# Four graph layers on one core: folding a weight product in the first layer and moving its softmax beside the aggregation

## Chip, cores and metric

One core of one Trainium2 chip runs the whole program. The metric is the time of one execution on the device in microseconds (us).

## What is computed

Four graph layers over N = 1536 nodes of 512 features, each followed by a residual sum and a layer norm. The change is in the first. With A the adjacency counts (24,576 edges and a loop at each node), it is:

```python
node_proj = h @ Wf + bf                       # 1536 x 256
img_proj = img_feats @ Wi + bi                # 36 x 256
logits = tanh(node_proj[:, None] + img_proj) @ Wa + ba
att = softmax(logits, axis=1)                 # 1536 x 36
img = att @ img_feats                         # 1536 x 1024
h1 = h @ Wn + bn
msg = A @ h1 + img @ Wim + bim
out = relu(concatenate([msg, h1]) @ Wap + bap)
x = layernorm(x + out)
```

Then come a relational layer of two steps, five GIN steps and a weighted aggregation, which the change leaves alone.

## The kernel before

Nodes stand in 12 tiles of 128 (`NT`), features in 4 blocks of 128. The program is written by hand, one instruction stream per engine: `block.sync` (SP) issues nearly all DMAs, `block.gpsimd` makes constants, `block.vector` (DVE), `block.scalar` (ACT) and `block.tensor` (PE) compute. Each stream runs in the order of its text and waits on semaphores (`wait_ge`); nothing else sets the order.

First come the edges: 96 windows of 16 nodes, in which one-hot matrices on DVE and products on PE make the adjacency matrices. Beside them the bases of the relational layer come in 64 chunks through four buffers (SP line 317) and are mixed on PE (L1205). The change touches the SP stream's last chunks.

The first layer follows, in four stretches:

1. `x_turned`: x is loaded three tiles at a time, transposed on PE (L1251) and copied to `xt` (L644). `projected` makes node_proj transposed (L1266), DVE copies it to `proj` (L661). ACT squares the rows of x for a bound (L1018). `pbias` holds the image's projection plus the biases.
2. PE makes G = img_feats Wim (L1387), then, per tile, h1 = x Wn (`rows`, L1295). DVE adds bn (L750), and splits h1 into two fp16 halves with a common scale (L752, L754). PE transposes h1 back (L1402), DVE copies it over `xt` (L757), since the output needs h1 as the stationary operand.
3. `aggregate` (L1309): per tile 24 fp16 products sum A h1. DVE scales it and adds bim (L771); PE transposes that message (L1434), DVE copies it (L776), and PE makes the output as own part (L1295) plus message part (L1441) in one bank; DVE adds bap into `xt` (L783).
4. When all lots (below) are summed, softmax for all 1536 nodes: `logit_t` (L787), transposes (L1447), max, exp, sum, transposes back (L1452). Then per tile the attended image, att times (G Wap's upper half), is made in its own bank (L1459), added (L810), relu and residual (L813), statistics (L814, L815), norm (L1064), transposed (L1473), copied (L1069).

The logits are made in 27 lots (`LOTS`): three groups of 512 nodes times nine sets of four image regions. ACT takes tanh of the upper 128 of the 256 features for the four regions (L1049), then of the lower (L1054). DVE's `halves` scales the upper (L733) and adds the lower with its weight (L739). PE's `dots` sums over the partitions (L1377), four products into four strips of 32 rows. `upper` is one buffer, `lower` two. DVE makes one lot per two tiles in stretch 2 and two per tile in stretch 3; PE does the same a tile or more later:

```python
# TensorE, stretch 2, after rows() of tile i and before the transposes of tile i - 1
if i >= 4 and i % 2 == 0:
    dots()
# VectorE, stretch 2, after shift and split of tile i and the copy of tile i - 1
if i >= 2 and i % 2 == 0:
    halves(1)
```

After stretch 4 the relational layer begins with its gates (L1334).

Of the kernel before, what the change touches and what calls it, by code (L numbers as in the profile page):

```python
# [8 lines left out]
P = 128  # L9
N, D = 1536, 512  # L10
NT = N // P
# [19 lines left out]
BB_COUNT = {3: 3, 4: 4, 5: 4, 6: 5, 7: 5, 8: 6}  # L31
MEASURED = (0, 2, 4, 5, 6, 7)
N_SMALL = 5 + 4
# [10 lines left out]
def program(nc, ins, out):  # L44
    with ExitStack() as ctx:
# [20 lines left out]
        wa = sb("wa", [P, 2], F32)  # L66
        pbias = sb("pbias", [P, 2, RG], F32)
# [28 lines left out]
        wim = part(hflat, 0, [8, D])  # L96
        wi = part(hflat, 16384, [8, PJ])
        proj = part(hflat, H1, [2, N])
        x_first = part(hflat, H1, [9, D])
        att_t = part(hflat, H1 + 12288, [N])  # L100
        img = part(hflat, H1 + 18432, [1024])
        g2 = part(hflat, H1 + 18432, [D])
        g_t = part(hflat, H1 + 20480, [4, RG])
        att = part(hflat, H1 + 22528, [NT, RG])
        wf = wb[:, 0, :, 0:PJ]

        adj_flat = [adj[:, m, :, :].rearrange("p j n -> p (j n)") for m in range(3)]
        logit_t = part(adj_flat[2], 0, [N])
        LOGIT = (2, 3, 7)
        LOTS = 3 * 9  # L110
        upper = part(adj_flat[2], 0, [4, 512])
        lower = [[part(adj_flat[2], 8192, [4, 512])], [part(hflat, H1 + 12288, [3, 512]), part(adj_flat[2], 16384, [1, 512])]]

        def lower_of(n, g):

            return lower[n % 2][0][:, g, :] if n % 2 == 0 or g < 3 else lower[1][1][:, 0, :]
# [78 lines left out]
        def static_slots(w):  # L195
# [6 lines left out]
        assert at <= 2 * 2 * NT * D  # L202
# [20 lines left out]
        weights = {k: sem("in_" + k) for k in ("wf", "wi", "img", "wim", "small", "wn", "wt", "wbm", "ts_out", "ts_in", "root", "l1a", "l1b", "aw", "att", "as_out", "as_in")}  # L223
# [9 lines left out]
        upper_ready, lower_ready, upper_scaled, halves_ready, halves_used = [sem(x) for x in (  # L233
            "upper_ready", "lower_ready", "upper_scaled", "halves_ready", "halves_used")]
# [3 lines left out]
        seen_ps, seen_read = sem("attended_ps"), sem("attended_read")  # L238
# [3 lines left out]
        h1_ready, h1t_ps, h1t_cp = sem("h1_ready"), sem("h1t_ps"), sem("h1t_cp")  # L242
        acc_ps, acc_read = sem("acc_ps"), sem("acc_read")
        m_ps, m_cp = sem("m_ps"), sem("m_cp")
# [16 lines left out]
        fin = sem("fin")  # L261

# [48 lines left out]
        def _(sp):  # L311
# [8 lines left out]
            for n in range(3):  # L320
# [9 lines left out]
                (epsc[:, 0:5], ins["L2_gnn_eps"].unsqueeze(0).broadcast_to([P, 5])),  # L330
            ]
# [4 lines left out]
            FIRST_SMALL = 8  # L336
            for n in range(CH):
# [70 lines left out]
            def first_of_l1():  # L408

                for k in range(4):  # L410
                    sp.wait_ge(comb_out[k], 64 * 17)
# [1148 lines left out]
```

## Time and profile before

| | before |
|---|---|
| median of 3 runs | 1946.56 us (1945.02 to 1951.14) |
| the profiled execution, own time | 1938.78 us |
| its span | 1937.0 us |
| mean granted clock of TensorE | 0.983 |
| PE busy | 1822.8 us (94%) |
| PEld, weight loads | 872.6 us (45%) |
| DVE busy | 860.6 us (44%) |
| ACT busy | 586.3 us (30%) |
| first stretch of the first layer to the relational layer's gates | 336.97 to 690.15 |

Busy time is the sum of the instructions' durations. A matmul's end is modelled, so where several follow each other their cost is the distance of their starts. A product in f32 appears as two records. Times in the rows are counted from the span's start.

### The profile page before, as it was taken

How to read it: one execution, taken by the hardware profiler on the slowest of the kernel's cores; microseconds unless marked ns; L12 is line 12 of the kernel's file. 1: busy time of each engine (PE TensorE's matmuls, PEld its weight loads, DVE VectorE, ACT ScalarE, POOL GpSimd, SP SyncE). 2: the span in 40 equal slices, each digit the busy share in tenths (PEclk: the TensorE clock that was granted, in tenths of full speed). 3: DMA queues.
4: the chain of work that ended last, by engine and by line, in shares of the span. 5: the costliest groups of instructions: out<-in, count | busy, mean ns of one | idle time of the engine just before them, and what ended most of it. 6: DMA issues, size and time to landing. Idle time of an engine off the chain costs nothing.

```text
span 1937.0 us, 22744 instructions
## 1 busy us (share of the span) xinstructions
PE 1822.8 (94%) x7442; PEld 872.6 (45%) x7454; DVE 860.6 (44%) x1956; ACT 586.3 (30%) x1179; POOL 8.0 (0%) x29
## 2 busy tenths in 40 slices
PE   5898887898999899999999999999999999999998
PEld 3555555343334344444444444454444445444443
DVE  7888786385664722010122222424343342584123
ACT  2555555246663421112111000232232323232100
POOL 1000000000000000000000000000000000000000
PEclk9999999999999699999999999999999999999999
DMA  7999988811000520000001011800000010021011
GB/s 185 241 263 254 236 226 213 327 50 39 0 1 0 185 109 19 25 0 1 22 0 55 33 33 47 338 1 1 28 1 28 1 38 1 1 71 60 22 55 44
DMA packets 46807, 157.50 MB, mean 81 GB/s; under 512 B 8746, under 2 KB 10690, under 8 KB 38246
## 3 DMA queue, kind: packets, MB, share of 16 engines
q1 hardware_dynamic: 42160, 142.27, 24.5%
q10 hardware_dynamic: 4534, 13.78, 1.9%
q8 instruction: 63, 1.03, 0.2%
q14 instruction: 50, 0.41, 0.1%
HBM read 120.38 MB, written 35.65 MB: 81 GB/s over the span
## 4 chain that ended last, share of the span: by engine, by line
PE 70%; DVE 9%; DMA 7%; ACT 5%; issue 4%; DVEq 3%; SPq 1%; another core or an unknown queue 1%; POOL 0%; ACTq 0%; POOLq 0%
PE psum L1309 28%; PE psum L1295 27%; PE psum L1540 6%; DMA hs<-in_L_gnn_basis 4%; ACT adj L1049 2%; PE psum L1491 2%; DVE adj L739 2%; ACT adj L1054 1%; PE psum L1205 1%; PE psum L1459 1%; DMA adj<-in_L_gnn_basis 1%; PE psum L1226 1%; ACT hs L1054 1%; DMA wb<-in_L_gnn_Wn 1%; DVE hs L612 1%
## 5 line engine op out<-in xcount | busy, mean ns | idle before, releaser
L1309 PE MATMUL psum<-hs,adj 128*128 128x512 f16 x2880 | 638.0, 379 | 1.5 <-DVE hs L764 1.5
L1295 PE MATMUL psum<-wb,xt 128*128 128x512 f32 x1152 | 506.4, 597 | 3.7 <-DVE hs L903 3.4
L1309 PEld LDWEIGHTS psum<-hs,adj 128*128 128x128 f16 x2880 | 280.8, 98 | 343.4 <-issue 20.9
L1295 PEld LDWEIGHTS psum<-wb,xt 128*128 128x128 f32 x1152 | 217.5, 192 | 264.1 <-issue 264.1
L1091 ACT ACTIVATE ua<-ua 128x512 f32<-128x512 f32 x60 | 37.8, 629 | 332.3 <-DVE ua L912 184.6
L844 DVE TENSOR_TENSOR vt<-psum,adj 128x512 f32<-128x512 f32 x24 | 16.6, 692 | 271.9 <-PE psum L1295 271.9
L908 DVE SCALAR_TENSOR_TENSOR vt<-psum,scl,xt 128x512 f32<-128x512 f32 x60 | 44.9, 749 | 199.7 <-PE psum L1309 199.7
L1540 PE MATMUL psum<-hs,adj 128*128 128x512 f32 x288 | 123.8, 592 | 0.0
L1049 ACT ACTIVATE adj<-hs,pbias 128x512 f32<-128x512 f32 x108 | 69.1, 710 | 93.7 <-DVE adj L739 93.7
L1079 ACT ACTIVATE lnst<-lnst,bcol 128x1 f32<-128x1 f32 x24 | 7.1, 295 | 282.1 <-DVE lnst L824 282.1
L838 DVE SCALAR_TENSOR_TENSOR hs<-psum,gates,hs 128x512 f16<-128x512 f32 x48 | 33.8, 747 | 121.0 <-ACT hs L1110 121.0
L1295 PE MATMUL psum<-adj,xt 128*128 128x512 f32 x192 | 86.3, 592 | 0.0
L1540 PEld LDWEIGHTS psum<-hs,adj 128*128 128x128 f32 x288 | 54.7, 190 | 68.9 <-issue 68.9
L901 DVE SCALAR_TENSOR_TENSOR xt<-psum,scl,hs 128x512 f32<-128x512 f32 x60 | 45.1, 751 | 87.8 <-ACT hs L1127 87.6
L988 ACT ACTIVATE wb<-psum 128x384 f16<-128x384 f32 x96 | 47.2, 491 | 118.1 <-PE psum L1226 118.1
L1127 ACT ACTIVATE hs<-psum,scl 128x512 f16<-128x512 f32 x60 | 41.0, 687 | 138.0 <-PE psum L1295 130.3
L1226 PE MATMUL psum<-xt 128*128 128x192 f32 x308 | 76.7, 332 | 0.0
L1225 PE MATMUL psum<-xt 128*128 128x384 f16 x154 | 51.4, 334 | 22.1 <-DVE xt L613 21.4
L1226 PE MATMUL psum<-hs 128*128 128x192 f32 x288 | 71.4, 330 | 0.0
L1110 ACT ACTIVATE hs<-psum,gates 128x512 f16<-128x512 f32 x48 | 30.4, 683 | 122.2 <-PE psum L1295 121.5
L932 DVE TENSOR_TENSOR vt<-psum,hs 128x512 f32<-128x512 f32 x12 | 8.3, 692 | 122.1 <-PE psum L1540 122.1
L611 DVE TENSOR_SCALAR xt<-hs 128x128 f32<-128x128 f16 x154 | 44.1, 286 | 41.4 <-PE psum L1226 24.1
(241 smaller groups left out, 1913.4 us busy)
## 6 DMA issues: line engine op xcount, KB each, us to landing
hs<-in_L_gnn_basis SPq DMA_DIRECT2D x38, 960.0 KB, 13.8
adj<-in_L_gnn_basis SPq DMA_DIRECT2D x26, 960.0 KB, 16.5
aw_scratch<-xt ACTq DMA_DIRECT2D x12, 768.0 KB, 9.2
adj<-aw_scratch SPq DMA_DIRECT2D x1, 9216.0 KB, 36.4
x_scratch<-adj SPq DMA_DIRECT2D x24, 256.0 KB, 2.1
hs<-x_scratch SPq DMA_DIRECT2D x24, 256.0 KB, 2.6
ts_scratch<-adj SPq DMA_DIRECT2D x1, 4608.0 KB, 23.3
as_scratch<-adj SPq DMA_DIRECT2D x1, 4608.0 KB, 16.9
```

The costliest lines, as they stand in the source:

```text
L611: dve.tensor_scalar(onehot_s[k], iota_s[:, 0:P], ecol[:, 0, bass.ds(t, 1)], None, ALU.is_equal)
L739: x = dve.scalar_tensor_tensor(v, v, wa[:, 1:2], upper[:, g:g + groups, :], ALU.mult, ALU.add)
L901: dve.scalar_tensor_tensor(own(i), psum[:, U_BANK[i % 3], :], scl[:, 2:3], kit["bb"][:, r % 2, :], ALU.mult, ALU.add)
L908: step(dve.scalar_tensor_tensor(vt[:, :], psum[:, i % 2, :], scl[:, 1:2], own(i), ALU.mult, ALU.add))
L988: act.activation(typed[:, s % 2, :, :, W * u:W * u + W], win[b][:, 0, 0:TW].rearrange("p (d m j) -> p m j d", d=W, m=2), ACT.Copy)
L1049: x = act.activation(upper[:, g, :], proj[:, 0, 512 * c:512 * c + 512], ACT.Tanh, bias=pbias[:, 0, 9 * g + a:9 * g + a + 1])
L1127: act.activation(hs[:, 0, 0, i, :], psum[:, U_BANK[i % 3], :], ACT.Copy, scale=scl[:, 0:1]).then_inc(u_hi, 1)
L1225: pe.matmul(win[b][:, 0, 0:TW], onehot_s16[k], onehot_t[k], start=first, stop=True, skip_group_check=True)
L1226: pe.matmul(win[b][:, 1, 0:AWW], onehot_s[k], onehot_w[k], start=first, stop=True, skip_group_check=True).then_inc(onehot_free[k], 1)
L1295: x = pe.matmul(psum[:, bank, :], xt[:, i, k, :], w[:, k, :], start=first and k == 0, stop=last and k == 3)
L1309: x = pe.matmul(psum[:, i % 2 + (4 * half if own else 0), :], adj[:, m, j, P * i:P * i + P], hs[:, t, half, j, :], start=n == 1 or (own an ...
L1540: x = pe.matmul(psum[:, i % 2, :], aw[:, j, P * i:P * i + P], sup[:, j, :], start=j == 0, stop=j == NT - 1)
```

## The change

Wn is multiplied into both halves of Wap first (`folded`: eight products of 128 rows, four for Wn times the upper half, into `wb`, four for Wn times the lower half, into `wb_top`), after 16 transposes of Wn. Then A x (Wn Wt) is aggregated and x (Wn Wb) is the own part, both from the same `xt`: h1 is neither transposed nor kept, and the message is neither transposed nor multiplied. bn and bim enter as columns (`bcols`), bn Wt is one product into `vt`, the rest goes into `g2`.

The attended image is one more product in the own part's bank; DVE scales the aggregation and adds the bank, so each tile's relu, statistics and norm can follow at once. The square roots of the norm are taken in groups. Softmax goes per group of 512 nodes, in steps after certain lots. In a lot there are two buffers for the first half and one for the second. The first lots stand in the fold. x is loaded in groups of 5 (ahead of the last basis chunks), 4 and 3 tiles into its own place, adjacency 2 is stored in two parts, and the weights of the fold go into free memory on SP's queue. Cut to what the prediction speaks of:

```diff
+                if n == CH - 3:
+                    x_load(2)
...
+            x_load(0)
+            x_load(1)
+            sp.dma_start(wi, ins["L0_gnn_Wi"].rearrange("(k p) n -> p k n", p=P)).then_inc(weights["wi"], 16)
+            sp.wait_ge(side_ps, len(side))
+            sp.wait_ge(typed_summed, BLOCKS)
+            sp.dma_start(wf, ins["L0_gnn_Wf"].rearrange("(k p) n -> p k n", p=P)).then_inc(weights["wf"], 16)
             sp.wait_ge(side_out, side_copied(len(side) - 1))
-            sp.dma_start(ts_dram, adj_flat[2]).then_inc(weights["ts_out"], 16)
+            sp.dma_start(ts_dram[:, 0:TS_HALF], adj_flat[2][:, 0:TS_HALF]).then_inc(weights["ts_a"], 16)
+            wap = ins["L0_gnn_Wap"].rearrange("(h k p) n -> h p k n", h=2, p=P)
+            sp.dma_start(wt, wap[0]).then_inc(weights["wt"], 16)
+            sp.dma_start(ts_dram[:, TS_HALF:], adj_flat[2][:, TS_HALF:]).then_inc(weights["ts_b"], 16)
+            sp.wait_ge(weights["ts_b"], 16)
+            sp.dma_start(wim, ins["L0_gnn_Wim"].rearrange("(k p) n -> p k n", p=P)).then_inc(weights["wim"], 16)
+            sp.dma_start(wbm, wap[1]).then_inc(weights["wbm"], 16)
...
+            def halves():
+                n = n_halves[0]
+                if n == LOTS:
+                    return
+                n_halves[0] += 1
+                dve.wait_ge(first_ready, n + 1)
+                for v in halves_at[n % 2]:
+                    x = dve.tensor_scalar(v, v, wa[:, 0:1], None, ALU.mult)
+                x.then_inc(first_scaled, 1)
+                dve.wait_ge(first_scaled, n + 1)
+                dve.wait_ge(second_ready, n + 1)
+                g = 0
+                for v in halves_at[n % 2]:
+                    groups = v.shape[1]
+                    x = dve.scalar_tensor_tensor(v, second[:, g:g + groups, :], wa[:, 1:2], v, ALU.mult, ALU.add)
+                    g += groups
+                x.then_inc(halves_ready, 1)
...
+            def folded(f):
+                dve.wait_ge(fold_ps, f + 1)
+                to = wb[:, 0, f, :] if f < 4 else wb_top[:, f - 4, :]
+                x = dve.tensor_copy(to, psum[:, FOLD_BANK[f % 3], :])
+                x.then_inc(fold_cp, 1)
+                if f < 4:
+                    dve.wait_ge(fold_cp, f + 1)
+                    dve.tensor_tensor(squares4[:, f, :], to, to, ALU.mult).then_inc(sq_ready, 1)
...
+            halves()
+            folded(0)
+            folded(1)
+            halves()
+            folded(2)
+            folded(3)
+            halves()
...
+            for i in range(NT):
+                dve.wait_ge(u_ps, i + 1)
+                if i >= 2:
+                    dve.wait_ge(u_lo, i - 1)
+                dve.tensor_tensor(ua[:, i % 2, :], psum[:, U0_BANK[i % 4], :], vt[:, :], ALU.add).then_inc(shifted, 1)
+                dve.wait_ge(shifted, i + 1)
+                dve.tensor_scalar(hs[:, 0, 0, i, :], ua[:, i % 2, :], scl[:, 0:1], None, ALU.mult).then_inc(u_hi, 1)
+                dve.wait_ge(u_hi, i + 1)
+                dve.scalar_tensor_tensor(hs[:, 0, 1, i, :], ua[:, i % 2, :], scl[:, 0:1], hs[:, 0, 0, i, :], ALU.mult, ALU.subtract).then_inc(u_lo, 1)
+                if i == 0 or i % 3:
+                    halves()
...
             for n in range(LOTS):
                 c, a = divmod(n, 9)
+                if a == 0:
+                    act.wait_ge(proj_cp, 2 * c + 2)
+                if n >= 2:
+                    act.wait_ge(halves_used, n - 1)
+                for g in range(4):
+                    x = act.activation(first_of(n, g), proj[:, 0, 512 * c:512 * c + 512], ACT.Tanh, bias=pbias[:, 0, 9 * g + a:9 * g + a + 1])
+                x.then_inc(first_ready, 1)
                 if n:
                     act.wait_ge(halves_ready, n)
                 for g in range(4):
-                    x = act.activation(upper[:, g, :], proj[:, 0, 512 * c:512 * c + 512], ACT.Tanh, bias=pbias[:, 0, 9 * g + a:9 * g + a + 1])
-                x.then_inc(upper_ready, 1)
-                if n >= 2:
-                    act.wait_ge(halves_used, n - 1)
-                for g in range(4):
-                    x = act.activation(lower_of(n, g), proj[:, 1, 512 * c:512 * c + 512], ACT.Tanh, bias=pbias[:, 1, 9 * g + a:9 * g + a + 1])
-                x.then_inc(lower_ready, 1)
-            act.wait_ge(logit_ready, 1)
-            act.activation(att, att, ACT.Exp).then_inc(exp_ready, 1)
+                    x = act.activation(second[:, g, :], proj[:, 1, 512 * c:512 * c + 512], ACT.Tanh, bias=pbias[:, 1, 9 * g + a:9 * g + a + 1])
+                x.then_inc(second_ready, 1)
...
+            def folded(f):
+                if f >= 3:
+                    pe.wait_ge(fold_cp, f - 2)
+                w = wt if f < 4 else wbm
+                for k in range(4):
+                    x = pe.matmul(psum[:, FOLD_BANK[f % 3], :], wn_t[:, k, P * (f % 4):P * (f % 4) + P], w[:, k, :], start=k == 0, stop=k == 3)
+                x.then_inc(fold_ps, 1)
...
+            pe.wait_ge(wnt_cp, 4)
+            pe.wait_ge(proj_cp, 4)
+            dots()
+            pe.wait_ge(weights["wt"], 16)
+            folded(0)
+            folded(1)
+            dots()
+            folded(2)
+            folded(3)
+            dots()
+            pe.wait_ge(proj_cp, 6)
...
+            for i in range(NT):
+                if i >= 4:
+                    pe.wait_ge(u_lo, i - 3)
+                rows(U0_BANK[i % 4], i, wb[:, 0, :, :]).then_inc(u_ps, 1)
+                if i == 0 or i % 3:
                     dots()
...
+            for i in range(NT):
+                if i >= 2:
+                    pe.wait_ge(acc_read, tick(0, i - 2))
+                aggregate(0, i, [0], between=between)
+                if i == 5:
+                    softmax_turn(2)
+                if i == 6:
+                    softmax_back(2)
+                if i == 7:
+                    colnorms(2, range(8), squares8)
+                if i >= 7:
+                    turned_back(2 * (i - 7))
+                pe.wait_ge(att_cp, i // 4 + 1)
+                if i >= 2:
+                    pe.wait_ge(o_read, tick(0, i - 2))
+                rows(4 + i % 2, i, wb_top, last=False)
+                pe.matmul(psum[:, 4 + i % 2, :], att_t[0:RG, P * i:P * i + P], g2[0:RG, :], start=False, stop=True).then_inc(o_ps, 1)
+                dots()
+                if i >= 7:
+                    turned_back(2 * (i - 7) + 1)
```

What the engines' orders look like where the lots meet the rest. TensorE before, from the start of stretch 2 (L1295: product with Wn; L1402: transposes of h1; L1377: a lot):

```order
L1387 MATMUL psum<-hs,img_t 36x512 x8
L1295 MATMUL psum<-wb,xt 128x512 x8
L1402 MATMUL psum<-ident,ua 128x128 x4
L1407 MATMUL psum<-ident,hs 128x36 x4
L1295 MATMUL psum<-wb,xt 128x512 x4
L1402 MATMUL psum<-ident,ua 128x128 x4
L1295 MATMUL psum<-wb,xt 128x512 x4
L1402 MATMUL psum<-ident,ua 128x128 x4
L1295 MATMUL psum<-wb,xt 128x512 x4
L1377 MATMUL psum<-adj,one_pad 32x512 x4
```

TensorE in the change, from the end of the fold (L1529: fold; L1515: a lot; L1417: product with the folded weight; L1494: transposes of logits):

```order
L1529 MATMUL psum<-hs 128x512 x4
L1515 MATMUL psum<-adj,one_pad 32x512 x4
L1417 MATMUL psum<-wb,xt 128x512 x4
L1515 MATMUL psum<-hs,one_pad 32x512 x3
L1515 MATMUL psum<-adj,one_pad 32x512
L1417 MATMUL psum<-wb,xt 128x512 x4
L1515 MATMUL psum<-adj,one_pad 32x512 x4
L1494 MATMUL psum<-ident,hs 128x128 x4
L1417 MATMUL psum<-wb,xt 128x512 x4
```

The first lot stood after the fifth tile's product; now a lot stands after every product, or every second one, and between the folds too.

VectorE before, the tile i = 2 of stretch 2 with its lot, and the next tile:

```order
L750 TENSOR_TENSOR ua<-psum,vt 128x512
L752 TENSOR_SCALAR hs<-ua,scl 128x512
L754 SCALAR_TENSOR_TENSOR hs<-ua,scl,hs 128x512
L757 COPY xt<-psum 128x512
L733 TENSOR_SCALAR adj<-adj,wa 128x2048
L739 SCALAR_TENSOR_TENSOR adj<-adj,wa 128x2048
L750 TENSOR_TENSOR ua<-psum,vt 128x512
```

VectorE in the change, the first tiles after the fold (L877, L879, L881: shift and split; L812, L819: a lot; L780: softmax):

```order
L812 TENSOR_SCALAR adj<-adj,wa 128x2048
L819 SCALAR_TENSOR_TENSOR adj<-adj,wa 128x2048
L877 TENSOR_TENSOR ua<-psum,vt 128x512
L879 TENSOR_SCALAR hs<-ua,scl 128x512
L881 SCALAR_TENSOR_TENSOR hs<-ua,scl,hs 128x512
L812 TENSOR_SCALAR hs<-hs,wa 128x1536
L812 TENSOR_SCALAR adj<-adj,wa 128x512
L819 SCALAR_TENSOR_TENSOR hs<-adj,wa,hs 128x1536
L819 SCALAR_TENSOR_TENSOR adj<-adj,wa 128x512
L780 TENSOR_SCALAR hs<-psum,bcol 128x512
L877 TENSOR_TENSOR ua<-psum,vt 128x512
```

Before, VectorE's lot of tile 2 was used by TensorE after tile 4's product. Now VectorE's lot stands behind the shift and split of the same tile after whose product TensorE asks for it.

## Rows read from the trace of the kernel before

**Rows 1.** Busy time in four stretches (length; busy time and instructions of PE, PEld, DVE, ACT, POOL; clock; DMA; GB/s).
```profile
336.97:378.99 42.02, 33.50 (x125) 16.93 (x127) 12.94 (x22) 10.46 (x29) 0.00 (x0) 1.00 0.82 313
378.99:446.80 67.81, 63.72 (x213) 26.34 (x212) 55.91 (x79) 30.19 (x49) 0.38 (x1) 1.00 0.30 112
446.80:631.88 185.08, 178.08 (x704) 71.97 (x704) 99.56 (x87) 104.57 (x168) 0.00 (x0) 0.98 0.00 1
631.88:690.15 58.27, 49.40 (x119) 21.41 (x121) 40.32 (x96) 25.15 (x46) 0.00 (x0) 0.65 0.48 162
```

**Rows 2.** Timeline of PE, third stretch (start, length, engine, line, operation).
```profile
482.69 0.66 PE L1434 MATMUL psum<-ident,ua 128*128 128x128 f32 x4
483.19 3.60 PE L1295 MATMUL psum<-wb,xt 128*128 128x512 f32 x8
486.62 3.60 PE L1441 MATMUL psum<-wb,adj 128*128 128x512 f32 x8
490.06 2.75 PE L1309 MATMUL psum<-hs,adj 128*128 128x512 f16 x12
492.74 1.07 PE L1377 MATMUL psum<-adj,one_pad 128*32 128x512 f32 x8
493.74 2.76 PE L1309 MATMUL psum<-hs,adj 128*128 128x512 f16 x12
```

**Rows 3.** Timeline of ACT, third stretch, in brackets the idle time before.
```profile
594.82 2.56 ACT L1049 ACTIVATE adj<-hs,pbias 128x512 f32<-128x512 f32 x4 [2.49 <-DVE adj L739]
...
602.44 2.56 ACT L1049 ACTIVATE adj<-hs,pbias 128x512 f32<-128x512 f32 x4 [2.62 <-DVE adj L739]
```

**Rows 4.** Timeline of DVE, second stretch: one tile's shift and split, one lot.
```profile
389.72 0.69 DVE L750 TENSOR_TENSOR ua<-psum,vt 128x512 f32<-128x512 f32 x1 [2.88 <-PE psum L1295]
...
390.97 0.75 DVE L754 SCALAR_TENSOR_TENSOR hs<-ua,scl,hs 128x512 f16<-128x512 f32 x1
...
400.10 1.28 DVE L733 TENSOR_SCALAR adj<-adj,wa 128x2048 f32<-128x2048 f32 x1
401.42 2.35 DVE L739 SCALAR_TENSOR_TENSOR adj<-adj,wa 128x2048 f32<-128x2048 f32 x1
```

**Rows 5.** Timelines of PE and DVE, end of the projections and second stretch.
```profile
377.25 0.69 DVE L661 COPY hs<-psum 128x512 f32<-128x512 f32 x1 [2.74 <-PE psum L1266]
...
385.98 7.13 PE L1295 MATMUL psum<-wb,xt 128*128 128x512 f32 x16
...
438.49 1.06 PE L1377 MATMUL psum<-adj,one_pad 128*32 128x512 f32 x8 [0.89 <-DVE adj L739]
```

**Rows 6.** Timeline of DVE: first and last of the scale's 12 small operations.
```profile
379.80 0.15 DVE L678 TENSOR_REDUCE scl<-norm 128x1 f32<-128x12 f32 x1
...
383.12 0.17 DVE L697 TENSOR_SCALAR scl<-scl_i 128x2 int32<-128x2 int32 x1
```

**Rows 7.** The chain that ended last (start, length, piece).
```profile
319.20 8.69 DMA hs<-in_L_gnn_basis
```

**Rows 8.** Busy time in two more stretches, columns as in rows 1.
```profile
305.00:310.00 5.00, 4.27 (x17) 2.40 (x17) 0.57 (x3) 0.60 (x1) 0.00 (x0) 0.66 0.99 272
...
650.00:660.00 10.00, 9.55 (x20) 3.65 (x18) 8.47 (x21) 5.56 (x11) 0.00 (x0) 0.50 0.53 173
```

**Rows 9.** Timeline of PE around three idle stretches.
```profile
464.28 1.08 PE L1377 MATMUL psum<-hs,one_pad 128*32 128x512 f32 x3 [3.86 <-DVE adj L739]
...
466.14 1.12 PE L1434 MATMUL psum<-ident,ua 128*128 128x128 f32 x4
467.05 5.00 PE L1295 MATMUL psum<-wb,xt 128*128 128x512 f32 x8
471.89 3.60 PE L1441 MATMUL psum<-wb,adj 128*128 128x512 f32 x8
...
634.64 1.53 PE L1447 MATMUL psum<-ident,adj 128*128 128x128 f32 x12 [2.76 <-DVE adj L787]
639.84 2.12 PE L1452 MATMUL psum<-ident,hs 128*36 128x128 f32 x12 [3.67 <-DVE hs L797]
```

More of the change, by code:

```diff
@@ new lines, in _ @@
+            dve.wait_ge(g_ps, 1)
+            dve.tensor_copy(g2[0:RG, :], psum[0:RG, 0, :]).then_inc(g_cp, 1)
+            halves()
+            folded(4)
+            dve.wait_ge(gt_ps, 1)
+            for q in range(4):
+                x = dve.tensor_scalar(g_t[:, q, :], psum[:, 0, RG * q:RG * q + RG], bcols[:, 1, q:q + 1], None, ALU.add)
+            x.then_inc(gt_ready, 1)
+            folded(5)
+            halves()
+            folded(6)
+            halves()
+            dve.wait_ge(weights["bap"], 16)
@@ new lines, in _ @@
+            dve.wait_ge(g2_ps, 1)
+            dve.tensor_tensor(g2[0:RG, :], psum[0:RG, 1, :], bap[0:RG, :], ALU.add).then_inc(g2_ready, 1)
+            halves()
+            folded(7)
+            halves()
+            for i in range(NT):
[8 more added lines that the diff above has]
+                if i == 0 or i % 3:
+                    halves()
@@ new lines, in _ @@
+            pe.wait_ge(wnt_cp, 4)
[9 more added lines that the diff above has]
+            pe.wait_ge(proj_cp, 6)
+            colnorms(0, range(4), squares4)
+            pe.wait_ge(weights["small"], 16 * N_SMALL)
+            for k in range(4):
+                x = pe.matmul(psum[:, 1, :], bcols[:, 0, k:k + 1].broadcast_to([P, P]), wt[:, k, :], start=k == 0, stop=k == 3)
@@ L1455, in attended @@
[L1455 to L1468 removed]
+            dots()
@@ new lines, in _ @@
+            pe.wait_ge(weights["wbm"], 16)
+            folded(4)
+            pe.wait_ge(g_cp, 1)
+            for k in range(4):
+                x = pe.transpose(psum[:, 0, RG * k:RG * k + RG], g2[0:RG, P * k:P * k + P], ident[0:RG, 0:RG])
+            x.then_inc(gt_ps, 1)
+            folded(5)
+            dots()
+            folded(6)
+            dots()
+            pe.wait_ge(gt_ready, 1)
+            pe.wait_ge(ct_ready, 1)
+            for k in range(4):
+                pe.matmul(psum[0:RG, 1, :], g_t[:, k, :], wt[:, k, :], start=k == 0, stop=False)
@@ new lines, in _ @@
+            for k in range(4):
+                x = pe.matmul(psum[0:RG, 1, :], bcols[:, 0, k:k + 1].broadcast_to([P, RG]), wbm[:, k, :], start=False, stop=k == 3)
+            x.then_inc(g2_ps, 1)
+            dots()
+            folded(7)
+            dots()
+            pe.wait_ge(fold_cp, 8)
+            pe.wait_ge(g2_ready, 1)
+            for i in range(NT):
[3 more added lines that the diff above has]
+                if i == 0 or i % 3:
+                    dots()
```

565 lines of the change are left out of this document (270 added, 295 removed).

## The prediction

> **What bounds the kernel now.** The change touches only the first layer, so I cut that layer out of the trace with the table of busy time by stretches [rows 1]: from the first transpose of x to the end of the projections 42.02 us, the product h1 = x Wn (with the image's projection ahead of it) 67.81, aggregation and output 185.08, softmax, attended image and norm 58.27; in all 353.18 us of the span of 1937.0. TensorE is busy in nearly all of it, though in the last stretch at a mean granted clock of 0.65. Next I read TensorE's timeline in the third stretch [rows 2]: a product of one tile (8 records) takes 3.44 us from start to start, 12 aggregation products 2.68, a lot's four products 1.00. The lot (tanh of 4 x 512 nodes in two halves, L1049 and L1054, then the weighting on VectorE, L733 and L739) repeats every 7.62 us on ScalarE [rows 3], since there is one buffer for the upper half. VectorE's timeline in the second stretch [rows 4] gives the two costs that matter most below: a tile's shift and split (L750, L752, L754) 389.72 to 391.72, 2.00 us, and a lot's two operations 400.10 to 403.77, 3.67 us; the tile's shift begins 0.31 us after its product's last start (385.98 + 3.43 = 389.41 [rows 5]).
>
> **What the order does.** All engines run their rows in order. Before, TensorE asks for a lot one tile (third stretch) or two (second) after VectorE's place for it: its first lot stands after the fifth tile's product, VectorE's stands with the third tile's. The trace shows what this buys: near the end of the stretch TensorE waits 0.89 us for a lot [rows 5], and in the steady third stretch hardly at all [rows 2]. In the changed order the distance is nil: TensorE has product, lot, product, lot, and VectorE has evacuation of that product, then that lot. So while TensorE waits for lot n, VectorE still evacuates the product just ended and then makes lot n; and the next product can't be evacuated before TensorE has it, which stands behind lot n. The two engines take turns. That is my forecast's reason.
>
> **The sum, in five parts** (full clock first). Hand-over from TensorE to VectorE 0.31, back 0.1.
>
> A, to the first lot on TensorE. x in another order, Wf behind about as many bytes on SP's queue, projections and Wn's 16 transposes in place of x's last 12: I leave the 42.02 us and add one thing. VectorE evacuates the last projection at 377.25 to 377.94 [rows 5] and only then makes lot 0: 377.94 + 3.67 + 0.1 = 381.7. So 44.8 us.
>
> B, the fold. Steps between lots, each with the lot's 1.00 on TensorE and the lot's 3.77 (3.67 + 0.1) on VectorE. Two with two folds: 1.00 + 6.88 + 0.31 + copy and square 1.38 (0.69 each, as the copy L661 [rows 5]) + 3.77 = 13.3, twice 26.7. One with the column norms and bn Wt: 1.00 + 4.3 + 0.31 + 0.69 + the scale's chain 3.49 (379.80 to 383.29 [rows 6]) + 3.77 = 13.6. Two with a product of 6.88 (G and g2): 12.65 each, 25.3. One with fold, transposes, fold: 13.0. Two with one fold: 9.2 each, 18.4. Sum 97.0 us, of which TensorE works 54.
>
> C, the product x (Wn Wt). Nine steps with a lot: 1.00 + 3.44 + 0.31 + 2.00 + 3.77 = 10.5, so 94.7; three tiles without one, 10.3. Sum 105.0 us, of which TensorE works 50.
>
> D, aggregation and output. Twelve tiles of 24 aggregation products (5.2), own part 3.44 and attended image 0.86 (a quarter of a tile's product) = 114.0; nine lots 9.0; transposes (0.44 for four) and column norms 7.9. Waits for lots in the first five tiles: VectorE makes the lot after the previous tile's sum, relu, statistics (2.4) and hand-over, 6.4 us after that tile's output, and TensorE reaches it after 1.00 + 2.68: 2.7 us each for four, 1.3 for the first, 12.1. Sum 143.0. The message's transposes and its product with Wap (3.43 and 0.6 a tile) are what this part no longer has.
>
> E, the tail. Softmax and attended sums are done in D; what remains is the last tile's norm beside the next layer's first product: 6.87 + transposes, copies and hand-overs 2.7 = 9.6, in place of 58.27.
>
> A to E are 399.4 against 353.2: **+46**. Costed at nothing: the DMAs of the fold's weights (the waits of B hide them; without those they would be due around 375), the store of adjacency 0 (4.6 MB, now beside aggregation, needed 500 us later), the tanh of ScalarE (2 x 2.56 a lot [rows 3], under steps of 9 to 13 us).
>
> Two more terms. **SP's queue**: the load of five x tiles (1280 KB) now stands ahead of the last basis chunk, for which TensorE waits already (8.69 us from issue [rows 7]). At the 272 GB/s that such loads reach [rows 8] it is 4.7 us; ends 0 and 4.7, I take 3.5, near the upper end since that chunk ends the wait. **The clock**: the trace shows an idle stretch of 3.86 us, after which lot and product ran at half clock in part (the lot 1.86 instead of 1.00, transposes 0.91 instead of 0.50, product 4.84 instead of 3.43: 2.7 us lost [rows 2, 9]), one of 3.67 that did the same, and one of 2.76 that did not [rows 9]. B and C have 17 waits of 4.7 us or more (10.5 - 4.44 = 6.1 in a step of C). Ends: 0, and 17 x 2.7 = 46. I take 30, since every wait is longer than the two that lost the clock, but where in the product it comes back varies. The skill says more: by the Trainium skill, TensorE: Matmul & The Clock Gate, section HAM oscillation, a loop whose wait is long enough starts every pass cold, all passes alike. By that rule the sum would be 16 us higher. The trace has too few such gaps to settle it.
>
> 46 + 3.5 + 30 = +79.5. Other layers stay as they are. The profiled execution took 1938.78 us (span 1937.0) and would take 2018; the median of the runs shown, 1946.56, lies 7.8 above it, so I forecast **2026 us** as a median.
>
> **Rivals.** 1. *The clock holds.* The turns are as above, but activity in them suffices: 1946.6 + 49.5 = 1996. For it: a gap of 2.76 did nothing, and at 0.89 nothing happened. Against: both gaps above 3.6 lost it. 2. *Every gap costs in full*: 17 x 2.7, 1946.6 + 49.5 + 46 = 2042. The skill's rule above is this case. For it: the row of 3.86. 3. *The clock stays low all through B and C*, as it did from 650 to 660, 0.50 with TensorE busy for 9.55 of 10 us [rows 8]: TensorE's 104 us of work in them double, 1946.6 + 49.5 + 104 = 2100. Against: full 128-row products follow each gap, and after 464.28 the clock came back within a product or two. 4. *VectorE isn't in the way* (the other side): if each lot were ready when TensorE asks, B is 54, C is VectorE's 12 x 2.00 + 9 x 3.67 = 57, D 131; with A 42 and E 9.6 that is 294 against 353, 1946.6 - 60 + 3.5 = 1890. It decides where VectorE's lot stands ahead of the evacuation that TensorE's next product feeds; the printed order says it doesn't, and VectorE would need to be one lot ahead in all 18 steps. For it: the lot's own cycle falls from 7.62 to about 5 us with the new buffers, and the tail of 58 us does go. 5. *The terms cancel*: turns cost less than I count (4 us a step less) and it ends within 0.3% of before.
>
> **Numbers.** Forecast (2010 to 2034) 0.50; rival 1 0.16; rival 2 0.18; rival 3 0.06; rival 4 0.06; rival 5 0.02; the last 0.02 is other slowdowns. A measurement of this kernel tells about 0.3% from no change. Faster 0.06, same 0.02, slower 0.92. Range 1988 to 2052: it leaves out rivals 3 to 5 and takes in the ends of the clock term and of SP's queue.
>
> **What would show it.** Right: TensorE in the fold and the product idle 4 to 6 us before each lot, released by VectorE's second lot operation, with VectorE idle in turn for TensorE's product; lots 10.5 us apart in C; a tail under 12 us; the gates' start near 770 (690.15 before); granted clock well below 1 in B and C (for rival 1: 1.0; for rival 3: 0.5 throughout). Wrong: lots 5 us apart on ScalarE from the start, TensorE without gaps there. Then rival 4 holds, and what I read as turns is hidden by a queue I don't see.

## The result, and the profile after

The changed kernel takes 2048.18 us (median of 4 runs, 2044.52 to 2050.36) against 1945.79 (4 runs, 1941.28 to 1951.14): the ratio is 1.0517, with a 95% interval of 1.0481 to 1.0553. The forecast was 2026 with a range of 1988 to 2052. The profiled execution took 2049.66 us (span 2047.8), 110.9 more than the one before.

| us | before | after | difference | forecast |
|---|---|---|---|---|
| to the first transposes of x | 336.97 | 351.72 | +14.75 | +3.5 |
| the first layer, to the gates | 353.18 | 449.31 | +96.13 | +76 (46 + 30 for the clock) |
| the rest of the span | 1246.85 | 1246.77 | 0 | 0 |

The new first layer by stretches, as in [rows 1] (A to the first lot, B fold, C product, D aggregation and output, E tail; B holds nine lots, from the one it starts with to the one ahead of C's first product):

```profile
351.72:398.41 46.69, 35.24 (x139) 19.14 (x140) 18.77 (x28) 16.25 (x37) 0.00 (x0) 0.91 0.76 286
398.41:514.68 116.27, 74.81 (x183) 22.85 (x184) 43.73 (x56) 41.81 (x68) 0.38 (x1) 0.81 0.04 14
514.68:641.63 126.95, 74.48 (x181) 25.75 (x177) 60.26 (x75) 45.27 (x75) 0.00 (x0) 0.78 0.05 18
641.63:791.38 149.75, 140.46 (x548) 58.00 (x546) 74.41 (x113) 62.06 (x102) 0.00 (x0) 0.96 0.19 66
791.38:801.03 9.65, 8.10 (x26) 3.81 (x25) 3.42 (x14) 2.90 (x5) 0.00 (x0) 1.00 0.30 110
```

Where the last two stretches of before took 243.35 us, D and E take 159.40, 84 us less, with softmax beside the aggregation, the message's products gone and fewer of the lots among them. The loss is in B and C: they take 243 us where the second stretch of before took 68, and TensorE is idle in 94 of them, at a mean clock of 0.81 and 0.78. The page puts the idle time on the lots, all of it released by VectorE's second lot operation (the last columns: busy, mean ns | idle time before):

```profile
L1515 PE MATMUL psum<-adj,one_pad 128*32 128x512 f32 x138 | 42.7, 858 | 54.6 <-DVE adj L819 54.6
...
L1515 PE MATMUL psum<-hs,one_pad 128*32 128x512 f32 x78 | 21.5, 916 | 52.7 <-DVE adj L819 52.7
```

The chain that ended last now has a longer piece for a basis chunk than [rows 7]:

```profile
327.53 12.88 DMA hs<-in_L_gnn_basis
```

One step of the product stretch, in TensorE's timeline and then in VectorE's and ScalarE's, shows the turns:

```profile
567.81 1.94 PE L1515 MATMUL psum<-adj,one_pad 128*32 128x512 f32 x8 [5.68 <-DVE adj L819]
569.68 5.80 PE L1417 MATMUL psum<-wb,xt 128*128 128x512 f32 x8
581.41 1.07 PE L1515 MATMUL psum<-hs,one_pad 128*32 128x512 f32 x3 [5.93 <-DVE adj L819]
```

```profile
565.40 2.35 DVE L819 SCALAR_TENSOR_TENSOR adj<-adj,wa 128x2048 f32<-128x2048 f32 x1
575.52 0.69 DVE L877 TENSOR_TENSOR ua<-psum,vt 128x512 f32<-128x512 f32 x1 [7.76 <-PE psum L1417]
...
576.77 0.75 DVE L881 SCALAR_TENSOR_TENSOR hs<-ua,scl,hs 128x512 f16<-128x512 f32 x1
...
580.61 0.75 DVE L819 SCALAR_TENSOR_TENSOR adj<-adj,wa 128x512 f32<-128x512 f32 x1
```

```profile
567.79 2.56 ACT L1151 ACTIVATE adj<-hs,pbias 128x512 f32<-128x512 f32 x4 [11.49 <-DVE adj L819]
...
581.39 2.56 ACT L1151 ACTIVATE adj<-hs,pbias 128x512 f32<-128x512 f32 x4 [8.39 <-DVE adj L819]
```

VectorE ends the lot at 567.75, TensorE sums it and makes the product, VectorE is idle for 7.76 us until that product ends, then evacuates it (575.52 to 577.52) and makes the next lot, while TensorE is idle for 5.93. The two engines' work does not overlap. ScalarE waits for the same lots, 11.49 and 8.39 us, since its buffer for a lot's second half comes free with them. The step is 13.60 us long, not 10.5, since the lot took 1.87 in place of 1.00 and the product 5.7 in place of 3.44: the first part of what TensorE does after each wait runs at half clock (1.2 GHz of 2.4). Below, "cold" stands for this.

Aggregation waits less. Of its four waits the two of 2.54 us are followed by half clock, those of 2.06 and 2.10 are not; one of each:

```profile
660.76 1.06 PE L1515 MATMUL psum<-adj,one_pad 128*32 128x512 f32 x8 [2.06 <-DVE adj L819]
661.75 2.77 PE L1431 MATMUL psum<-hs,adj 128*128 128x512 f16 x12
...
675.24 1.07 PE L1515 MATMUL psum<-adj,one_pad 128*32 128x512 f32 x8 [2.54 <-DVE adj L819]
676.24 4.45 PE L1431 MATMUL psum<-hs,adj 128*128 128x512 f16 x12
```

Ahead of the layer, the last basis chunk comes late: TensorE waits 5.75 us for it, where the kernel before waited 1.57 for the chunk of [rows 7], and again there is half clock behind the wait (a lot's eight records took 1.06 ahead of it):

```profile
331.72 1.06 PE L1317 MATMUL psum<-hs,attw 120*32 120x512 f32 x8
...
340.54 1.93 PE L1317 MATMUL psum<-hs,attw 120*32 120x512 f32 x8 [5.75 <-DMA hs<-in_L_gnn_basis]
```

### The profile page after: what moved, and what is told of

Same layout as the page of the kernel before. It is cut to its first block, busy times and chain, and to the rows that moved or that the text cites. A ratio compares the mean times of both kernels' runs of the same rounds, so it can differ in the third digit from the quotient of the medians.

```text
span 2047.8 us, 22538 instructions
## 1 busy us (share of the span) xinstructions
PE 1837.2 (90%) x7346; PEld 868.4 (42%) x7358; DVE 852.5 (42%) x1957; ACT 584.0 (29%) x1171; POOL 8.0 (0%) x29
## 4 chain that ended last, share of the span: by engine, by line
PE 78%; DVE 9%; DMA 8%; issue 3%; DVEq 1%; ACT 1%; POOL 0%; POOLq 0%
PE psum L1431 29%; PE psum L1417 29%; PE psum L1686 6%; DMA hs<-in_L_gnn_basis 4%; DMA adj<-in_L_gnn_basis 3%; PE psum L1515 2%; DVE adj L819 2%; PE psum L1529 2%; PE psum L1637 2%; PE psum L1317 2%; PE psum L1338 2%; PE psum L1377 1%; PE psum L1337 1%; DVE adj L812 1%; DVE hs L819 1%
## 5 line engine op out<-in xcount | busy, mean ns | idle before, releaser
L1417 PE MATMUL psum<-wb,xt 128*128 128x512 f32 x1056 | 474.5, 610 | 3.4 <-DVE hs L1001 3.4
L1417 PEld LDWEIGHTS psum<-wb,xt 128*128 128x128 f32 x1056 | 205.3, 197 | 264.3 <-issue 264.2
L1417 PE MATMUL psum<-adj,xt 128*128 128x512 f32 x288 | 129.5, 593 | 0.0
L1515 PE MATMUL psum<-adj,one_pad 128*32 128x512 f32 x138 | 42.7, 858 | 54.6 <-DVE adj L819 54.6
L1417 PEld LDWEIGHTS psum<-adj,xt 128*128 128x128 f32 x288 | 54.3, 190 | 55.8 <-issue 51.6
L1515 PE MATMUL psum<-hs,one_pad 128*32 128x512 f32 x78 | 21.5, 916 | 52.7 <-DVE adj L819 52.7
```

Source lines behind the costliest of these rows:

```text
L1417: x = pe.matmul(psum[:, bank, :], xt[:, i, k, :], w[:, k, :], start=first and k == 0, stop=last and k == 3)
L1515: x = pe.matmul(psum[32 * g:32 * g + 32, LOGIT[c], :], one_pad[:, 31 - a:63 - a], first_of(n, g), start=a == 0, stop=a == 8)
```

## Experiments

All times are medians; beside each stands the ratio to the kernel before, run on the same chip, with its interval. "One lot behind" is the theory of turns made into an edit. The kernel before has a median of its own beside each run: 1942.76 us (e_lag, e_fill, e_x_late, e_small_late), 1945.80 (e_dve_first, e_x_behind, e_b_small, e_best) and 1946.95 (e_fold_lag). So a difference of two medians from different lines, or from the changed kernel's, can be off by up to 4 us.

| run | us | ratio (interval) |
|---|---|---|
| e_lag | 1899.48 | 0.9768 (0.9742 to 0.9794) |
| e_dve_first | 1985.76 | 1.0203 (1.0170 to 1.0235) |
| e_fold_lag | 1990.56 | 1.0220 (1.0203 to 1.0237) |
| e_fill | 2029.65 | 1.0444 (1.0418 to 1.0471) |
| e_x_late | 2043.83 | 1.0519 (1.0491 to 1.0548) |
| e_x_behind | 2042.46 | 1.0490 (1.0457 to 1.0524) |
| e_small_late | 2047.23 | 1.0536 (1.0509 to 1.0562) |
| e_b_small | 1949.22 | 1.0009 (0.9990 to 1.0028) |
| e_best | 1889.89 | 0.9711 (0.9685 to 0.9736) |

**TensorE one lot behind.** One call of `dots()` is left out; the softmax steps follow by one lot.

```diff
             pe.wait_ge(proj_cp, 4)
-            dots()
             pe.wait_ge(weights["wt"], 16)
...
-                    if n == 9 * c + 9:
+                    if n == 9 * c + 10:
                         softmax_turn(c)
```

> The changed kernel with one thing more: TensorE asks for each lot one place later (its first place for a lot, after the projections, is left out, and the softmax steps of VectorE and ScalarE move one lot later with it); VectorE and ScalarE make the lots where they did. Theory 'turns' (TensorE's and VectorE's places stand at distance nil, so each waits for the other): the fold falls from 116 us to 55 to 65, the product stretch from 127 to 60 to 70 (12 x 2.00 + 9 x 3.67 = 57 on VectorE is then its floor), the waits before lots from 5.7-6.0 us to under 1.5, aggregation loses its four waits of 2.1 to 2.5, and the clock is near 1 again: 2048 - 52 - 60 - 9 = about 1927, range 1905 to 1950. Rival 'the lots are too slow for the short stretches' (ScalarE's 5.1 us and VectorE's 3.7 us per lot set the pace, wherever TensorE asks): steps stay at 9 to 10.5 us and the time falls by the clock's share alone, to 2000 to 2030. Rival 'clock' (half clock is what stretches the two parts): waits vanish but products stay at 4.3 to 5.8 us, about 1970.

Measured: 1899.48 us, 149 less than the changed kernel (146 when each is taken against the kernel before beside it) and 43 less than before. That is 5.5 us below the forecast's range: fold and product each gained 8 us more than I had said, and the first stretch 4.6, which I had left out. The stretches:

```profile
391.95:447.89 55.94, 55.31 (x176) 18.41 (x175) 44.20 (x58) 36.58 (x58) 0.38 (x1) 1.00 0.08 29
447.89:506.47 58.58, 53.11 (x180) 19.66 (x177) 56.19 (x70) 45.65 (x74) 0.00 (x0) 1.00 0.02 2
506.47:645.00 138.53, 135.90 (x555) 56.83 (x553) 80.60 (x121) 67.61 (x111) 0.00 (x0) 1.00 0.25 87
```

(first stretch 42.06 us, tail 9.65.) The fold falls to 55.94 us, the product to 58.58, with a clock of 1.00. In the product stretch VectorE now hardly stops (its longest idle time there is 0.78 us):

```profile
457.57 0.69 DVE L877 TENSOR_TENSOR ua<-psum,vt 128x512 f32<-128x512 f32 x1
...
459.48 1.28 DVE L812 TENSOR_SCALAR adj<-adj,wa 128x2048 f32<-128x2048 f32 x1
460.80 2.35 DVE L819 SCALAR_TENSOR_TENSOR adj<-adj,wa 128x2048 f32<-128x2048 f32 x1
```

TensorE waits 0.4 to 1.2 us there for a lot, for VectorE's 2.00 + 3.67 us a step are the pace. The same instructions, the same buffers, the same work: the layer takes 304.76 us in place of 449.31, so the places cost 145 us. This was the 'turns' row of the expectation; neither rival held, since steps with one product fell below 6 us and products are back at 3.44.

**The same distance made on VectorE, in the product stretch alone:**

```diff
             for i in range(NT):
+                if i == 0 or i % 3:
+                    halves()
                 dve.wait_ge(u_ps, i + 1)
...
-                if i == 0 or i % 3:
-                    halves()
```

> The changed kernel with VectorE's lot ahead of the tile's shift and split in the product stretch alone; TensorE's order stays. It is the same distance of one, made on the other engine. Theory 'turns': the product stretch falls from 127 us to 60 to 72 (VectorE makes the lot while TensorE makes the product), the fold stays at 116 us with its waits of 5.3 to 6 us: 2048 - 60 = 1988, range 1978 to 2000. Rival 'it was the missing first lot' (what the run with TensorE one lot behind gained came from less work ahead of the stretch or from the softmax steps moved): the stretch stays over 100 us, 2030 or more.

**And on TensorE in the fold alone** (its first `dots()` left out, and one more after `folded(7)`):

> The changed kernel with TensorE one lot behind in the fold alone; the lot is caught up at the fold's end, so that the product stretch has its old order. Theory 'turns, stretch by stretch': the fold falls from 116 us to 56 to 62 and the product stretch stays at 125 to 128: 2048 - 57 = 1991, range 1984 to 1998; with VectorE's lot moved forward in the product stretch alone the time was 1985.8, so the two gains add up to what the lag in both brought (1899.5). Rival 'one clock': what the clock loses in one stretch it would have lost in the other; then the gains overlap and this run is above 2005.

Measured 1985.76 and 1990.56. With VectorE's lot forward the fold is as it was and the product stretch falls:

```profile
395.02:510.90 115.88, 74.77 (x184) 22.68 (x184) 45.05 (x58) 41.82 (x68) 0.38 (x1) 0.81 0.04 14
510.90:577.33 66.43, 56.93 (x181) 20.74 (x177) 56.10 (x71) 44.96 (x74) 0.00 (x0) 0.94 0.00 0
```

With the fold's lag the fold takes 61.66 us (391.89 to 453.55) and the product stretch stays at 127.69:

```profile
453.55:581.24 127.69, 75.21 (x181) 26.03 (x177) 60.26 (x75) 45.45 (x75) 0.00 (x0) 0.78 0.05 18
```

The gains are 62.4 and 57.6 us, 120 of the 149. Of the other 29, aggregation is 11.2 (149.75 to 138.53, since the lag takes most of its waits too), the product stretch 7.9 (58.58 with the lag, 66.43 with VectorE's lot forward, where three waits of 2.24 to 2.25 stay and two lots run cold) and the fold 5.7 (55.94 against 61.66, in which the lot is caught up after a wait of 3.98); the last 4 lie within what medians from different lines can be off. The distance can be made on either engine, and in each stretch by itself; the rival of one clock, which would have shown 2005 or more, falls.

**More work, less time.** Four f32 products ahead of eight of the nine waits in the product stretch, into a bank that nothing reads:

```diff
-            def dots():
+            def dots(fill=0):
...
+                for k in range(fill):
+                    pe.matmul(psum[:, 0, :], ident[:], wb[:, 0, k % 4, :], start=True, stop=True)
```

> The changed kernel with work added: ahead of eight of the nine waits for a lot in the product stretch TensorE makes four f32 products (identity times the folded weight, into bank 0, which nothing reads), 3.44 us of it at full clock, inside a wait of 5.7 to 6.0 us. Theory 'the clock is lost in the waits': the idle time before a lot falls to about 2.6 us, lots and products after it run at full clock (0.83 to 1.0 and 3.44 us in place of 1.9 and 4.3 to 5.8), the steps go from 12.6-13.4 us to 10.5-11.0, and the stretch from 127 us to 107 to 112: the kernel with more work is 15 to 20 us faster, 2028 to 2033. Rival 'turns cost it all, the clock nothing': steps stay, or grow by what does not fit, 2048 to 2060.

Measured 2029.65 us, 18.5 less with 28 us of work more (15.5 less when each is taken against the kernel before beside it). The product stretch is 16.3 us shorter:

```profile
512.20:622.85 110.65, 85.64 (x244) 33.37 (x241) 60.24 (x75) 45.27 (x75) 0.00 (x0) 0.95 0.06 20
```

Two of its steps (L1510 is the added product, L1517 the lot):

```profile
534.60 1.07 PE L1517 MATMUL psum<-adj,one_pad 128*32 128x512 f32 x8 [2.25 <-DVE adj L819]
...
536.09 3.60 PE L1417 MATMUL psum<-wb,xt 128*128 128x512 f32 x8
539.53 3.60 PE L1510 MATMUL psum<-wb,ident 128*128 128x512 f32 x8
545.62 0.63 PE L1517 MATMUL psum<-hs,one_pad 128*32 128x512 f32 x3 [2.50 <-DVE adj L819]
```

The step from lot to lot is 11.02 us with the softmax's transposes (0.49) in it, 10.5 without: the forecast's step to a tenth. So the turns are 10.5 us, and the other 2 to 3 us of a step were the clock's. Two of the eight filled waits still cost some (the products behind them took 5.24 and 8.67 us, not 3.44 and 6.97). The one step left unfilled waits 5.93 us and runs cold again.

**The queue ahead of the layer.** x's last five tiles, three of which the new order transposes first, loaded behind the edge work (e_x_late), then only behind the last chunk's load (e_x_behind, shown):

```diff
-                if n == CH - 3:
-                    x_load(2)
...
                     load_chunk(follower(n))
+                if n == CH - 3:
+                    x_load(2)
```

> The changed kernel with the load of the five last x tiles (1280 KB) moved from ahead of the last basis chunk to behind the edge work. Theory 'the queue': the last basis lot, which came at 340.54 with a wait of 5.75 us, comes 4 to 5 us earlier (336 or so; the load moved is 1280 KB, 4.7 us at 272 GB/s), but the first x tiles in the new order then land later, so that the first transposes of x start where they did, give or take 3 us: the whole within 6 us, 2042 to 2050. Rival 'the lag is older': the basis chunks were already 8.15 us behind the kernel before at the issue before the x load (315.12 against 306.96), so at least 8 of the 14.75 us stay; under this the start of the first transposes stays above 345.

> The changed kernel with the load of the five last x tiles behind the last basis chunk's load instead of ahead of it (same place in the program, two lines swapped). Behind the edge work it bought 6.5 us on that chunk (last two lots 4.58 us apart in place of 8.82, then 2.25 us less at half clock) and lost most of it again in waits for x of 2.13, 2.53 and 3.49 us. Theory 'the queue in order': the last two lots are again about 4.6 us apart, the transposes of x follow without a wait for x over 1 us, and the whole is 5 to 7 us faster than the changed kernel, 2041 to 2043. Rival 'shared engines': the x load takes bandwidth from the chunk although it stands behind it, and the lots stay 7 to 9 us apart, 2046 to 2050.

Measured 2043.83 and 2042.46. The last two lots of the edge work are 4.58 us apart when x comes late, and 5.22 when it stands behind, in place of 8.82. The six profiled kernels with the load ahead have them 8.7 to 9.3 apart, and the kernel before in its three profiles 4.1 to 4.6.

```profile
328.88 1.07 PE L1316 MATMUL psum<-hs,attw 120*32 120x512 f32 x8
```

```profile
333.46 1.06 PE L1316 MATMUL psum<-hs,attw 120*32 120x512 f32 x8 [1.51 <-DMA hs<-in_L_gnn_basis]
```

```profile
328.95 1.06 PE L1317 MATMUL psum<-hs,attw 120*32 120x512 f32 x8
```

```profile
334.17 1.49 PE L1317 MATMUL psum<-hs,attw 120*32 120x512 f32 x8 [2.14 <-DMA hs<-in_L_gnn_basis]
```

Late, three waits for x (2.13, 2.53, 3.49 us) take the gain back: against the kernel before beside it, the run is 1.3 us better than the changed kernel. Behind, the only wait for x is 0.61, the layer starts at 344.73 and the run is 5.7 us better, as forecast. The load ahead of the chunk cost 4.24 us of transfer, near the 4.7 of [rows 8]'s rate, and 2.25 more at half clock after the longer wait (from the last lot to the next f16 transposes 5.73 us after, 3.48 with x late): 6.5 us, not 3.5. Behind the chunk it still costs 2.3 of them, since the last lot waits 2.14 us and runs cold in part (5.22 and 5.11 in place of 4.58 and 3.48).

**The two column loads.** bn and bim, 512 packets of four bytes each, moved behind the half store; and the reverse, added to the kernel before:

```diff
+                (bcols[:, 0, :], ins["L0_gnn_bn"].rearrange("(k p) -> p k", p=P)),
+                (bcols[:, 1, :], ins["L0_gnn_bim"].rearrange("(k p) -> p k", p=P)),
```

> The changed kernel with the two loads of bn and bim as columns (four bytes a packet) moved from among the basis chunks (82.56 and 87.19 us) to behind the half store of adjacency 2. Theory 'small packets': the basis chunks that fall behind the kernel before from 0.4 us at the 16th to 5 us at the 25th no longer do, the chunk issued at 315.12 comes 5 to 8 us earlier, and the whole is 2040 to 2043. Rival 'drift': the chunks are as late as they were (the lag of 4 to 8 us is how the DMA queues happened to run), and the time stays within 3 us of 2048. If the columns now come too late for bn Wt, TensorE waits there and some of the gain goes.

> The kernel before with the two loads of bn and bim as columns of four bytes a packet added among the basis chunks, where the changed kernel has them; nothing reads them. Theory 'small packets': the 25th chunk, which came at 120.35 in the kernel before and at 123.8 to 125.4 in three kernels with these loads, comes at 123 or later, the chunk that was issued at 306.96 comes 2 to 4 us later, and the whole is 2 to 4 us slower than before. Rival 'drift of the queues': it comes within 1.5 us of 120.35 and 306.96, and the time is the same within 0.15%.

The forecast for the first, 2040 to 2043 us, was missed, and the medians say little: 1.0 us less than the changed kernel (2.1 more when each is taken against the kernel before beside it), and 1949.22 against 1945.8 (the interval, -1.9 to +5.4 us, holds zero). To see how far the edge phase wanders by itself I profiled the kernel before twice more:

> The kernel before, unchanged, profiled again. The profiled execution of before took 1938.78 us, its 17 other executions 1939.8 to 1954.0 with median 1945.8. Theory 'the edge phase wanders': the chunk issued at 306.96 comes later here by about as much as the execution is longer (1945 us: near 313), and the first layer takes 353 us again. Rival 'the column loads cost it': with no such loads the chunk stays at 307 to 308, whatever the execution takes, and 3.6 to 8.2 us of lag belong to the change.

> The same once more, for the spread: by 'the edge phase wanders' the chunk's time and the whole move together, between 305 and 315 and between 1938 and 1951 us; by the rival the chunk stays within 1 us of 307.

They took 1944.32 and 1940.39 us. The chunk that before issued at 306.96 came at 310.81 and 307.38, so the phase does wander, by 4 us: less than the first theory said, more than its rival. But all eight profiles with the column loads among the chunks have it at 311.5 to 315.1 (mean 313.3), and all five without them at 304.7 to 310.8 (mean 308.1). The issue of that chunk in the changed kernel, and with the columns late:

```profile
315.12 0.33 SPq L349 DMA_DIRECT2D hs<-in_L_gnn_basis  x1
```

```profile
310.61 0.33 SPq L349 DMA_DIRECT2D hs<-in_L_gnn_basis  x1
```

The earlier sign that I had named, the chunk at 120.35, says nothing: without the loads it came at 121.63 and 124.62 in the two repeats. So the loads cost about 5 us at the later chunk. At the layer's start the two runs differ: moved away, they let it start at 346.92, 2.7 us before the mean of the kernels that keep them (below); added to the kernel before, they make it start at 342.74, 5.1 after that kernel's mean. The medians of the whole show none of it beyond their spread. By the Trainium skill, DMA: Bandwidth & Descriptors, section Why small descriptors are slow, every packet has a fixed cost beside its bytes. The rows here fit that, with 7595 packets under 512 bytes up to 340 us in place of 6605 and only 4 KB more to load, but no row prices a packet, so that the packets are the cause is argued. The two repeats of the kernel before start the layer at 339.90 and 336.16 (336.97 in the first profile), mean 337.7; the five kernels that share the changed queue up to there start it between 348.28 and 351.72, mean 349.7. So 12.0 of the 14.75 us are typical, and the rest is the draw. The x load's 6.5 and some 5 for the columns would make up the 12.0; the next run, with both moved, starts the layer at 337.71, where the kernel before does.

**All together:** one lot behind, x behind the chunk, columns late, and Wf loaded ahead of Wi.

```diff
-            sp.dma_start(wi, ins["L0_gnn_Wi"].rearrange("(k p) n -> p k n", p=P)).then_inc(weights["wi"], 16)
             sp.wait_ge(side_ps, len(side))
             sp.wait_ge(typed_summed, BLOCKS)
             sp.dma_start(wf, ins["L0_gnn_Wf"].rearrange("(k p) n -> p k n", p=P)).then_inc(weights["wf"], 16)
+            sp.dma_start(wi, ins["L0_gnn_Wi"].rearrange("(k p) n -> p k n", p=P)).then_inc(weights["wi"], 16)
```

> TensorE one lot behind, plus three edits of the queue: the load of the five last x tiles behind the last basis chunk's, the column loads of bn and bim behind the half store, and Wf loaded ahead of Wi (the first projection waited 4.0 us for Wf and then ran at half clock in part, 9.14 us in place of 7.13). The run with the lag alone took 1899.5. If the terms add: -6 for the x load, -1 to -3 for the columns, -4 to -6 for Wf: 1885 to 1890. If Wi then comes too late for the image's projection, or x for its transposes, 1890 to 1896.

Measured 1889.89 us (6 runs, 1886.51 to 1894.53), 2.9% under the kernel before and 7.7% under the changed one. The layer starts at 337.71 and takes 301.41 us:

```profile
337.71:376.08 38.37, 35.26 (x138) 19.00 (x139) 14.52 (x25) 16.14 (x36) 0.00 (x0) 0.96 0.91 344
376.08:432.38 56.30, 55.46 (x177) 18.41 (x175) 44.22 (x58) 36.51 (x58) 0.38 (x1) 1.00 0.10 29
432.38:490.93 58.55, 53.11 (x181) 19.66 (x177) 56.04 (x70) 45.59 (x74) 0.00 (x0) 1.00 0.01 2
```

The first stretch is 38.37 us in place of 42.06, and the terms added up as forecast (1885 to 1890). The change as a whole is worth having: e_lag, which alters only where a lot is asked for, is 43 us under the kernel before, and where TensorE asked for the lots was what lost. No run separates the fold, the merged output and the early softmax, nor tries the queue's order in the kernel before.

## Why the prediction was right, and where it was off

- **Turns (right).** The order rows said "distance nil", and e_lag, e_dve_first and e_fold_lag each took back the loss of its stretches by changing the distance alone. The signs named in advance came: waits of 4.4 to 6.0 us (8.3 once) before each lot in B and C, released by VectorE's second lot operation; VectorE idle for TensorE's product in turn; a tail under 12 us. The gates came at 801, not 770, and the lots of C 12.2 to 13.7 us apart where one product lies between, not 10.5, which are the two sizes below.
- **The sums of A to E (right within about 2 us each, at full clock).** TensorE's busy time in B is 74.81 us and in e_lag 55.31, with one lot (1.0 us) less in it; in C 74.48 and 53.11, for the same work; in D 140.46 and 135.90, where e_lag has that lot more. The clock is what is left: 18.5, 21.4 and 5.6. The forecast's parts hold 26 of the 27 lots; with the missing one, 1.0, put into B, its 98.0, 105.0 and 143.0 give 116.5, 126.4 and 148.6 with the clock; measured 116.27, 126.95 and 149.75. A was 46.69 (44.8): TensorE waits 4.15 us for Wf there, and the projection behind that wait takes 9.04 us, where the next one at full clock takes 7.13. E was 9.65 (9.6). In D I had the attended image at 0.86 and the own part at 3.44; they are 1.06 and 3.52, 3.4 us in twelve tiles, against waits of 9.2 in place of 12.1.
- **The clock term (the step that was most off).** "Ends: 0, and 17 x 2.7 = 46. I take 30, since [...] where in the product it comes back varies." It was 45.5 (18.5 + 21.4 + 5.6), and 1.9 more in A. The waits for lots are 18 up to the end of C, since one stands at the end of A. They cost 2.3 us each, not much less than my example's 2.7; 2.0 of that falls into the first products of D, behind the last wait of C. The two waits of 2.54 us in aggregation, where I had put none, cost 1.7 each. The three gaps of [rows 9] had already said so: both above 3.6 us lost it, and all of mine were longer. To average over "it varies" without a row that showed a long gap at no cost was the error. Rival 2 was the case; that its 46 is met so well is in part luck: 42 came from the waits that it counts, and 3.4 from aggregation. The rule I cited, the Trainium skill, TensorE: Matmul & The Clock Gate, section HAM oscillation, says that such a loop starts every pass cold; by that rule the sum would have been 16 us higher. In C the trace agrees: each of the lots behind its nine waits begins at half clock. In B it does not quite: the lots at 460.76 and 487.72, after waits of 4.35 and 4.37 us, took 1.38 and 1.05 us in place of 1.86, and the clock fell only behind them (next product 4.89 and 5.06).
- **SP's queue (too small a term, and one left out).** "I take 3.5", with ends 0 and 4.7. The load cost 6.5: the transfer was in the range (4.24), but the wait it made longer cost clock as well, and I had counted clock only for B and C. The two column loads, some 5 us by the chunk's time (3 to 5 at the layer's start), I did not cost at all: they are two lines in the list of small loads, and I looked for the waits they might cause, not at their packets.
- **The median.** I added 7.8 us because before's profiled execution lay that far under its median. After's lies 1.5 above its own. The difference of medians, 102.4, is therefore less than that of the profiles, 110.9, and hides some 8 us of the two errors. 2048.18 is in the range, near its end, and that is in part luck: 110.9 on top of before's median of 1945.79 would be 2056.7, beyond it.
- **Rivals.** 1 (the clock holds) is refuted by the clock of 0.81 and 0.78 in B and C, and by e_fill's gain. 3 (low throughout) by the same 0.78, where it said 0.5. 5 (the terms cancel) by the time itself. 4 (VectorE not in the way) was false of this kernel, but its condition, VectorE one lot ahead in all steps, is e_lag: it forecast 294 us for the layer, and e_lag took 304.76. Most of the difference is in D, 138.53 where it had 131.

## What to carry to other kernels

When two in-order engines feed each other twice in a loop (a product to evacuate one way, a piece to sum the other), write down for each piece how many places lie between the maker's place and the user's. At nil they take turns, and the step is the sum of both engines' work; at one it is the larger of the two. Here that was 10.5 us a step (12.2 to 13.7 with the clock that the waits cost) against 5.7, for one call left out. Cost every wait of several us on TensorE with the clock it loses afterwards, also waits that a DMA makes; and count a load's packets, not only its bytes.

## What the runs showed of the hardware

Adding 28 us of products that nothing reads made the kernel 15 to 18 us faster (2029.65 us), since they stood in waits of 5.7 to 6.0 us that otherwise halved the clock of what follows: the clock of the stretch rose from 0.78 to 0.95.

Length alone does not decide whether a short wait costs clock. In e_dve_first two waits of the same length had the opposite outcome for the same eight records, whose cost at full clock is 1.00 us (1.00 and 1.87 to the next start):

```profile
536.99 1.06 PE L1515 MATMUL psum<-adj,one_pad 128*32 128x512 f32 x8 [2.25 <-DVE adj L819]
...
553.11 1.93 PE L1515 MATMUL psum<-adj,one_pad 128*32 128x512 f32 x8 [2.24 <-DVE adj L819]
```

In the changed kernel's aggregation 12 products took 4.45 us after a wait of 2.54 and 2.77 after one of 2.06 (rows above), but in e_lag after one of 2.58 they took 2.76:

```profile
511.81 0.63 PE L1515 MATMUL psum<-hs,one_pad 128*32 128x512 f32 x3 [2.58 <-DVE adj L819]
...
512.81 2.76 PE L1431 MATMUL psum<-hs,adj 128*128 128x512 f16 x12
```

and in e_fill six of eight waits of 2.24 to 2.59 cost nothing. What settles it in that range stays open; no run here was made for it. Whether the spread of the column loads' cost (nothing to 1 us in one pair of medians, 3.4 in the other, 5 at the chunk) is the wandering of the edge phase or a later wait that hides it, stays open too.
